# Keeping the last expert step's output rows in SBUF and fetching them by SBUF to SBUF transfers

## The reference, cut to what matters

```python
x = L0_attn_x                                        # (1, 8192, 512), f32
x = _layernorm(x + _L0_attn_ref(x, ...))             # long convolution by FFT; three earlier phases
x = _layernorm(x + _L0_ffn_ref(x, ...))              # this phase

def _L0_ffn_ref(x, controller, f1, bias, f2):        # 32 tokens per group, 128 experts (32 x 4)
    grouped = x.reshape(B, g, t, d)                  # 256 groups of 32 tokens
    logits = einsum('bgtd,des->bgtes', grouped, controller) + tie
    perm = (logits == max(logits, axis=-3))          # per group and expert: the one token it takes
    dispatched = einsum('bgtd,bgtes->bgesd', grouped, perm)
    inner = relu(einsum('bgesd,desf->bgesf', dispatched, f1) + bias)
    intermediate = einsum('bgesf,esfd->bgesd', inner, f2)
    return einsum('bgesd,bgtes->bgtd', intermediate, perm)   # "combine"
```

## Time and profile before

| | us |
|---|---|
| median of 3 runs | 2304.3 (2299.67 to 2306.85) |
| the profiled execution | 2312.54 |
| its span | 2310.7 |
| busy in the span: PE, DVE, ACT, POOL | 1933.4, 1387.6, 949.0, 440.1 |
| step 1, layers (part of it) | 1780 to 1838 |
| step 3, layers | 2062 to 2160 |
| late stage, loads issued to last combine | 2166 to 2302 |

### The profile page before, as it was taken

The page is one execution under the profiler, slowest core; times in us unless marked ns, Lnnn a source line. Parts: engine busy times, 40 slices in busy tenths (PEclk is TensorE's granted clock), DMA queues, the critical chain, the costliest instruction groups (busy, mean ns, idle before and its releaser), DMA issues. The chain is left out here.

```text
span 2310.7 us, 35055 instructions
## 1 busy us (share of the span) xinstructions
PE 1933.4 (84%) x12598; PEld 1322.0 (57%) x12598; DVE 1387.6 (60%) x2672; ACT 949.0 (41%) x1756; POOL 440.1 (19%) x279
## 2 busy tenths in 40 slices
PE   5999999999999699999769999994767676576444
PEld 5777777777777344444359988883636362252000
DVE  3878777777777255555458888882443354354344
ACT  3444444444444344444345555554323232242222
POOL 1100010011000044444345554540000000000000
PEclk9999999999999799999979999996888887686655
DMA  4134233423332578888587777756797999989999
GB/s 144 65 110 136 102 110 110 142 101 110 117 130 92 174 202 222 221 220 223 160 258 239 243 245 225 238 185 240 251 398 270 393 345 407 406 302 409 372 392 341
DMA packets 300365, 522.65 MB, mean 226 GB/s; under 512 B 26943, under 2 KB 119263, under 8 KB 291874
## 3 DMA queue, kind: packets, MB, share of 16 engines
q1 hardware_dynamic: 290978, 503.63, 64.5%
q10 hardware_dynamic: 9216, 16.78, 1.9%
HBM read 314.50 MB, written 205.82 MB: 225 GB/s over the span
## 5 line engine op out<-in xcount | busy, mean ns | idle before, releaser
L89 PE MATMUL p_pu<-p_xT_high,p_win_high 128*128 128x512 f32 (+1 forms) x816 | 334.6, 410 | 23.7 <-POOL p_xT_low L84 23.5
L91 PE MATMUL p_pu<-p_xT_low,p_win_high 128*128 128x512 f32 (+1 forms) x816 | 318.3, 390 | 0.0
L90 PE MATMUL p_pu<-p_xT_high,p_win_low 128*128 128x512 f32 (+1 forms) x816 | 318.3, 390 | 0.0
L369 ACT ACTIVATE p_t<-p_pu,p_tbias,p_taps 128x512 f32<-128x512 f32 x192 | 149.4, 778 | 385.2 <-PE p_pu L91 384.1
L473 DVE SCALAR_TENSOR_TENSOR p_t<-p_halo,p_taps,p_t 128x128 f32<-128x128 f32 (+1 forms) x384 | 196.8, 517 | 137.0 <-ACT p_t L369 135.9
L473 DVE SCALAR_TENSOR_TENSOR p_t<-p_pu,p_taps,p_t 128x384 f32<-128x384 f32 (+1 forms) x384 | 210.2, 547 | 6.9
L751 POOL TENSOR_TENSOR q_y<-q_y 128x512 f32<-128x512 f32 x128 | 160.3, 1273 | 277.8 <-DVE q_y L778 277.8
L84 POOL TENSOR_TENSOR p_xT_low<-p_xT,p_xT_high 128x2048 fp32r<-128x2048 f32 (+1 forms) x17 | 77.2, 4541 | 626.0 <-ACT p_xT_high L79 626.0
L89 PEld LDWEIGHTS p_pu<-p_xT_high,p_win_high 128*128 128x128 f32 x816 | 155.0, 190 | 56.9 <-issue 29.4
L1427 DVE COPY e_taken<-e_pd 128x1024 f32<-128x1024 f32 x64 | 78.4, 1224 | 161.8 <-PE e_pd L1360 161.6
L91 PEld LDWEIGHTS p_pu<-p_xT_low,p_win_high 128*128 128x128 f32 x816 | 154.4, 189 | 34.6
(11 more groups left out here) (120 smaller groups left out, 3499.9 us busy)
## 6 DMA issues: line engine op xcount, KB each, us to landing
s_I<-e_out SPq DMA_DIRECT2D x64, 1024.0 KB, 8.2
s_SV<-p_sout SPq DMA_DIRECT2D x128, 256.0 KB, 2.0
q_av<-s_SV SPq DMA_DIRECT2D x64, 512.0 KB, 4.3
s_Z<-q_z SPq DMA_DIRECT2D x128, 256.0 KB, 3.2
o_zin<-s_Z SPq DMA_DIRECT2D x64, 512.0 KB, 3.6
e_ff<-in_L_ffn_f SPq DMA_DIRECT2D x64, 512.0 KB, 8.9
e_inter<-s_I SPq DMA_DIRECT2D x32, 1024.0 KB, 12.8
e_taken<-s_I SPq DMA_DIRECT2D x32, 1024.0 KB, 11.3
```

The source lines that it names most:

```text
L89: pe.matmul(out, a[0], b[0], start=start, stop=False)
L90: pe.matmul(out, a[1], b[0], start=False, stop=False)
L91: return pe.matmul(out, a[0], b[1], start=False, stop=stop)
L369: nc.scalar.activation(t[r][m % 2][:], pu[(W + n) % 3][:], ACT.Identity, bias=tbias[:, w:w + 1], scale=taps[:, w, 2:3]).then_inc(t_ok, 1)
```

## The change

The output rows of step 3 no longer go to `I`. `keep_out` copies them into `taken`, over the dispatched rows of the same quad, which layer 1 has read by then; `taken` has a new shape for this, [128, 16 quads, 2048], and the dispatched rows of a quad lie together in it. A partition of `taken` then holds, for one group, the rows of 64 experts, 128 KB.

A late tile takes the rows of the first 64 experts from `I` as before (`load_stored`, 512 KB, into partitions 0 to 63), and those of the other 64 by four transfers from SBUF to SBUF, one for each group: from the one partition of `taken` that holds the group to partitions 64 to 127, 64 rows of 2 KB, 128 KB. The four groups of a tile lie in four partitions that are 8 apart (`place`); so `keep_tile` writes a tile's four group columns 8 elements apart, in every step, and the loads from `I` take groups 8 rows apart.

The late slots can't be in `taken` any more. There are seven: the buffers `out`, `inter` and the weight buffers, with the selections in `pick` and the tokens in `res` and `xt`. Before them SP waits for the last combined tile's matmul and for all its stores to the output; ACT and DVE close tile 31 ahead of the late stage. For the first three late tiles the half from `I` is loaded in the middle of step 3's layers.

```diff
-        taken = sb("taken", [P, DT * EH * GH])
+        taken = sb("taken", [P, QH, 4 * D])
...
+        def place(t):
+            return slice(4 * SPREAD * (t % 4) + t // 4, 4 * SPREAD * (t % 4) + t // 4 + 3 * SPREAD + 1, SPREAD)
+        def of_tile(m):
+            at = place(m % TH)
+            return slice(m // TH * GH + at.start, m // TH * GH + at.stop, at.step)
...
-                sp.dma_start(inter[s][:], S["I"][4 * m:4 * m + 4].rearrange("g e d -> e g d")
+                sp.dma_start(inter[s][:], S["I"][of_tile(m)].rearrange("g e d -> e g d")
...
+            def load_stored(m):
+                s = (m - NT0) % NL
+                sp.dma_start(late[s][0:EH], S["I"][of_tile(m), 0:EH].rearrange("g e d -> e g d")).then_inc(late_in[s], 16)
             def load_late(m):
                 s = (m - NT0) % NL
                 if m >= NT0 + NL:
                     sp.wait_ge(c_ps, ONE + m - NL + 1)
                 tile, choice = inter_of(m)
-                sp.dma_start(tile, S["I"][4 * m:4 * m + 4].rearrange("g e d -> e g d")).then_inc(late_in[s], 16)
+                if m >= NT0 + NO:
+                    load_stored(m)
+                for g, p in enumerate(range(P)[place(m % TH)]):
+                    sp.dma_start(tile[EH:ES, g, :], taken[p:p + 1].rearrange("o i (e d) -> o (i e) d", e=4)
+                                 ).then_inc(late_in[s], 16)
...
-                    sp.dma_start(S["I"][g0:g0 + GH, 4 * q:4 * q + 4, :], out[n % NO][:]).then_inc(stored[n % NO], 16)
+                    if c < STEPS - 1:
+                        sp.dma_start(S["I"][g0:g0 + GH, 4 * q:4 * q + 4, :], out[n % NO][:]).then_inc(stored[n % NO], 16)
...
+                    if c == STEPS - 1 and i == QH // 2:
+                        for x in range(NO):
+                            sp.wait_ge(stored[x], stores_before(x, (STEPS - 1) * QH))
+                        for x in range(NO):
+                            load_stored(NT0 + x)
-            for x in range(NO):
-                sp.wait_ge(stored[x], stores_before(x, STEPS * QH))
-            for s in range(2):
-                sp.wait_ge(h_ps[s], ONE + STEPS * QH // 2)
+            sp.wait_ge(c_ps, ONE + NT0)
+            sp.wait_ge(tile_ps, ONE + STEPS * TH)
+            sp.wait_ge(o_ps, ONE + STEPS * QH)
+            for s in range(NR):
+                sp.wait_ge(res_st[s], ONE + 16 * NT0 // NR)
             for m in range(NT0, NT):
                 load_late(m)
...
-            copy(rows[:, :, :, t * 4:(t + 1) * 4].rearrange("p k e (h g) -> p (k e) h g", g=2),
-                 pd[:, n % ND].rearrange("p h k e g -> p (k e) h g")).then_inc(taken_ok[n % 2], 1)
+            copy(rows[:, :, :, :, place(t)].rearrange("p i k e (h g) -> p (i k e) h g", g=2),
+                 pd[:, n % ND].rearrange("p h i k e g -> p (i k e) h g")).then_inc(taken_ok[n % 2], 1)
...
+            if n < (STEPS - 1) * QH:
+                eng.wait_ge(stored[n % NO], ONE + n // NO * 16)
+                to = out[n % NO][:, 2 * b:2 * b + 2, :]
+            else:
+                to = taken[:, n % QH, 2 * b * D:2 * (b + 1) * D].rearrange("p (e d) -> p e d", e=2)
+            copy(to, po[b]).then_inc(o_ok[b], 1)
```

More of the change, by code:

```diff
@@ L1152, in experts_phase @@
     NT0 = NT // NH
-    NL = 8
-    LW = 5 * D + P
+    NL = 7
+    SPREAD = P // 16
     with ExitStack() as ctx:
@@ L1164, in experts_phase @@
         pick = [sb(f"pick{s}", [P, 2, 2 * EH]) for s in range(NP)]
-        ff = [sb(f"ff{s}", [P, 2, D]) for s in range(NF)]
+        weights = sb("ff", [P, NF, 2, D])
+        ff = [weights[:, s] for s in range(NF)]
         hid = [sb(f"hid{s}", [P, GH]) for s in range(2)]
@@ L1172, in experts_phase @@
         std = [sb(f"std{s}", [P, 1]) for s in range(2)]
-        pd = ctx.enter_context(nc.psum_tensor("e_pd", [P, ND, 2, DT, EH, 2], F32))
+        pd = ctx.enter_context(nc.psum_tensor("e_pd", [P, ND, 2, QH, DT, 4, 2], F32))
         pc = [ctx.enter_context(nc.psum_tensor(f"e_pc{s}", [P, D], F32)) for s in range(2)]
-        banks = pd[:].rearrange("p b h k e g -> p (b h) (k e g)")
+        banks = pd[:].rearrange("p b h i k e g -> p (b h) (i k e g)")
         po = [banks[:, 0:2, :], banks[:, 2:4, :]]
         ph = [banks[:, 4 + s, 0:GH] for s in range(2)]
-        rows = taken[:].rearrange("p (k e g) -> p k e g", k=DT, e=EH)
-        late = taken[:, 0:NL * LW].rearrange("p (s w) -> p s w", w=LW)
+        rows = taken[:].rearrange("p i (k e g) -> p i k e g", k=DT, e=4)
+        late = [t[:] for t in out + inter] + [weights[:, 2 * n:2 * n + 2].rearrange("p n a d -> p (n a) d") for n in range(2)]
+        late_take = [pick[s // 2][:, s % 2, :] for s in range(NL)]
+        late_own = [t[:] for t in res] + [t[:, a, :] for t in xt for a in range(2)]
         consts, eps_ok = sem("e_consts"), sem("e_eps_ok")
@@ L1209, in inter_of @@
                 return inter[m % NI][:], take[m % NI][:]
-            v = late[:, (m - NT0) % NL, :]
-            return v[:, 0:4 * D].rearrange("p (g d) -> p g d", g=4), v[:, 4 * D:4 * D + P]
+            return late[(m - NT0) % NL], late_take[(m - NT0) % NL]
         def res_of(m):
@@ L1216, in res_of @@
                 return res[m % NR][:]
-            return late[:, (m - NT0) % NL, 4 * D + P:5 * D + P]
+            return late_own[(m - NT0) % NL]
         def combined(c):
@@ L1323, in _ @@
                         load_tile(m + NI)
-            for x in range(NO):
-                sp.wait_ge(stored[x], stores_before(x, STEPS * QH))
-            for s in range(2):
-                sp.wait_ge(h_ps[s], ONE + STEPS * QH // 2)
+                    if c == STEPS - 1 and i == QH // 2:
[8 more added lines that the diff above has]
+                sp.wait_ge(res_st[s], ONE + 16 * NT0 // NR)
             for m in range(NT0, NT):
                 load_late(m)
-            for s in range(NR):
-                sp.wait_ge(res_st[s], ONE + 16 * NT0 // NR)
             for s in range(NL):
-                sp.wait_ge(late_st[s], ONE + 16 * (NT - NT0) // NL)
+                sp.wait_ge(late_st[s], ONE + 16 * len(range(s, NT - NT0, NL)))
         @block.gpsimd
@@ L1359, in dispatch @@
                             r = slice(h * 2 * GT, (h + 1) * 2 * GT)
-                            m = pe.matmul(pd[:, b, h, k].rearrange("p e g -> p g e"), x[r, a, k * P:(k + 1) * P],
-                                          chosen[r, a, :].rearrange("p (g e) -> p g e", g=2), start=True, stop=True)
+                            m = pe.matmul(pd[:, b, h, :, k].rearrange("p i e g -> p g i e"), x[r, a, k * P:(k + 1) * P],
+                                          chosen[r, a, :].rearrange("p (g i e) -> p g i e", g=2, e=4), start=True, stop=True)
                     m.then_inc(tile_ps, 1)
@@ L1372, in layer1 @@
                         m = pe.matmul(ph[s][r, :], ff[w][:, 0, k * P + e * EF:k * P + (e + 1) * EF],
-                                      rows[:, k, 4 * i + e, :], start=(k == 0), stop=(k == DT - 1))
+                                      rows[:, i, k, e, :], start=(k == 0), stop=(k == DT - 1))
                 m.then_inc(h_ps[s], 1)
@@ L1391, in combine @@
                 else:
-                    pe.wait_ge(late_in[(m - NT0) % NL], ONE + ((m - NT0) // NL + 1) * 32)
+                    pe.wait_ge(late_in[(m - NT0) % NL], ONE + ((m - NT0) // NL + 1) * 96)
                 if m >= 2:
@@ L1426, in keep_tile @@
                     eng.wait_ge(h_ps[s], ONE + c * QH // 2)
-            copy(rows[:, :, :, t * 4:(t + 1) * 4].rearrange("p k e (h g) -> p (k e) h g", g=2),
-                 pd[:, n % ND].rearrange("p h k e g -> p (k e) h g")).then_inc(taken_ok[n % 2], 1)
+            copy(rows[:, :, :, :, place(t)].rearrange("p i k e (h g) -> p (i k e) h g", g=2),
+                 pd[:, n % ND].rearrange("p h i k e g -> p (i k e) h g")).then_inc(taken_ok[n % 2], 1)
         def keep_out(eng, copy, b, n):
             eng.wait_ge(o_ps, ONE + n + 1)
-            eng.wait_ge(stored[n % NO], ONE + n // NO * 16)
-            copy(out[n % NO][:, 2 * b:2 * b + 2, :], po[b]).then_inc(o_ok[b], 1)
+            if n < (STEPS - 1) * QH:
[4 more added lines that the diff above has]
+            copy(to, po[b]).then_inc(o_ok[b], 1)
         @block.scalar
@@ L1452, in close @@
             def close(m):
-                if m:
+                if m and m != NT0:
                     finish(m - 1)
@@ L1467, in _ @@
                         close(m)
+            finish(NT0 - 1)
             for m in range(NT0, NT):
@@ L1525, in _ @@
                         normed(m)
+            scale(NT0 - 1)
             for m in range(NT0, NT):
```

## The result

The changed kernel took 2549.9 us (median of 4 runs, 2546.5 to 2554.9) against 2304.7: a ratio of 1.106, interval 1.104 to 1.108. I had forecast 2337, at most 2520. The sign was right; the loss is 245 us, seven and a half times the 33 that I forecast.

What follows compares the result with a forecast made beforehand. It took DMA traffic to bound step 3's layers and the late stage. From the profiled 2312.5 us, -30, 0, 0, -4 and +67 gave 2345.5; less 8.2 to the runs' median, 2337 us, range 2263 to 2520.

Steps and rivals of the forecast that it cites:

- What bounds the kernel: Step 3's layers and the late stage: DMA engines full, both as long as their bytes need.
- Part 1: Step 3's layers: removing 16 stores of 1 MB shortens them, -30 us, from -22 to -37.
- Part 2: Junction before the late stage: store wait gone, tile 31's output wait in its place, 0 us, from -2 to +5.
- Part 3: Copies into taken: single elements 8 apart cost nothing, 0 us, at most some +5.
- Part 4: Late stage: narrow transfers raise a tile from 4.26 to 6.4 us, +67 us; early half tiles -4 us.
- The term for width: Late stage: 64 partitions cost 1.05 us more per 256 KB, 4.2 us per tile if no other traffic fills the gap.
- C: Late stage: engines meet at one partition, transfer after transfer; 25 us per tile, 2930 us, chance 0.20 with everything above 2500.
- the floor of side by side: Late stage: a tile's four single-partition transfers run at the same time, at least 5.5 us per tile.
- the 25 us of one after another: Late stage: four transfers of 5.5 us in turn plus 2.9 us for the tile's other traffic.
- B: The forecast itself: contention in part in the late stage, 2337 us, own range 2298 to 2420, chance 0.45.
- Rival A: Late stage: single-partition transfers cost only their bytes, 4.26 us per tile, 2270 us (2281 if issues limit), chance 0.28.
- D: Step 3's layers: stores gone but no shorter, as PE and copies set the wait; 2367 us, chance 0.07.

Runs made afterwards that it cites:

- e3: Kernel before with only the new places of the groups, 8 apart in taken and in I; stores and late stage unchanged: 2320.1 us.
- e9: Kernel before without step 3's 16 stores and the waits for them, late tiles loading other rows of the same bytes: 2270.0 us.
- e14: Changed kernel with the halves from I of the first three late tiles loaded in the late stage: 2541.8 us.
- e1: Changed kernel, each SBUF to SBUF transfer reading 2 KB from each of 64 partitions, not 128 KB from one (wrong rows): 2366.2 us.
- e4: Kernel before with each late tile's 1 MB load from I split into two 512 KB loads to 64 partitions each: 2373.1 us.
- e6: Changed kernel with a tile's four groups in partitions t, t+32, t+64 and t+96, issued in that order: 2768.9 us.
- e12: Changed kernel with groups 32 partitions apart, issued in the order t, t+64, t+32, t+96: 2611.9 us.
- e7: Changed kernel with consecutive tiles taking their groups from the lower and the upper 64 partitions by turns: 2547.9 us.
- e2: Changed kernel with a tile's four groups in four neighbouring partitions in place of 8 apart: 2828.9 us.
- e8: Changed kernel with a tile's four single-partition transfers issued between its other loads: 2586.7 us.
- e5: Changed kernel with ACT issuing the transfers of a tile's third and fourth group on its own queue: 2503.6 us.

## Why the prediction was wrong

The sum, from the runs: layout +12 (e3), stores and their wait gone -35 (e9), the new wait at the junction +6, early halves +8 (e14; +4 by its trace), narrow destinations 32 x 2.07 = +66 (e1, e4), single sources 32 x 5.7 = +182 (e1). Together +239 of the 245 us measured. The two profiled executions lie 234 us apart (2546.54 against 2312.54), so the sum is good to some 10 us, not better.

**What bounds the kernel** held for the kernel before: e9 takes bytes out of the layers and they get shorter. In the late stage after the change the bytes no longer set the time, for hardly fewer take 2.8 times as long.

**Part 1** (-30, from -22 to -37): the mechanism was right, and the size for the stores alone: e9's layers are 29.5 us shorter. The changed kernel kept 22 of them, the small end of the range (4.7 us between quads, where I had named 4.2 as the sign), since three narrow loads went in front of the weights. I had counted these by their bytes, 1.6 MB or 4 us in the layers and -4 us in the late stage. They cost 8.2 us in the layers and saved 4.4 (e14), a net loss of 4 to 8 us.

**Part 2** (0): right. From the last copy to the first late issue 2151.03 - 2145.11 = 5.9 us, against 6.5 to 6.6 before. e9 has no wait there, which makes this wait's price the +6 of the sum. What I said of the first late tile is part of the 12.03 us per tile and was not measured apart.

**Part 3** (0, at most +5): wrong. "So stride costs nothing" rested on one row of 128 elements at distance 64 (347 ns), of another operation, that is not a copy of 1024 elements. The copies became 1.55 times as long on DVE and 1.9 times on ACT. "64 x 1.2 = 78 us fits in it" treated waiting summed over all stages as cover for each copy. It did cover most: in e3 the copies add 98 us of work to the two engines (120.9 against 78.4 and 120.1 against 64.3) and 12 to the time. By the time of step 3's first store e3 is 10.4 us late (2077.03 against 2066.64), while at step 1's it was only 2.2 us (1782.42 against 1780.19): most is lost in the dispatch of steps 2 and 3. From the last store of step 1 to the first of step 2 it takes 1913.14 - 1842.06 = 71.1 us against 1904.47 - 1837.44 = 67.0. There the combine's work lies on the same two engines, which would explain it; no run tests this.

**Part 4** is the step that failed: "I take 6.4 us per tile", measured 12.03. The term for width came out right (half of 4.2, that is 2.1; e4 2.0, e1 2.1), though no row had shown that it is half and not all. So my 6.4 is the time of a tile with wide sources (6.33 in e1), and the single source in effect stood in the sum at nothing. It costs 5.7 us per tile, 182 us in all. It was taken as hidden, with the reason that "seven slots and the queue let the engines be at different transfers at the same time". They do so hardly: the order of transfers within a tile changes its time from 18.7 to 13.9 us (e6, e12), the order of tiles nothing (e7). Nor does an engine that is a little ahead get further ahead, my argument against C. Four transfers of 4.7 us from four places took 5.7 us more than from wide sources. So the price is neither the floor of side by side, 5.5 us, nor the 25 us of one after another, but about a third of the way from the one to the other. I had both ends in the text and put the likeliest value at the low one. The range stopped at 2520, early in the gap between B (to 2420) and C (2930); all above 2500 had a chance of 0.20, under C. By my own sign, a late stage of over 280 us, the forecast was wrong: it is 385. **Rival A** fell, **D** too. **C** had the right mechanism (engines meet at one partition) and an overlap too few; with neighbouring partitions (e2) it comes nearly true.

## What to carry to other kernels

Where the DMA engines are full, count for each transfer how many partitions it reads and writes, not only its bytes: 1 MB into halves of 64 partitions cost 2 us more than into 128, and 128 KB out of one partition held the engines at some 28 GB/s while it ran alone. Here the bytes saved in one stage (35 us) did not pay for the narrow shape in another. And when two prices for an unseen operation lie far apart, the range must hold what lies between them, unless a row excludes it.

## What the runs showed of the hardware that I had not expected

- An engine's busy share does not tell what it moves: 0.86 at 131 GB/s in the changed kernel, 1.04 at 382 before.
- ACT and DVE copies of 1024 f32 to single places: with two of them in each 16 bytes nearly at full speed (1059 and 1228 ns), one per 16 bytes or farther 1.9 to 2.06 us. The Trainium skill, SBUF — State Buffer, section "Specifications (TRN2)", says that a cacheline is 16 bytes and wants two hits per line; here the border lies exactly there. Why 128 elements at distance 64 took no longer than 128 in one run stays open: at the 0.66 ns per element that the 1024 cost more, 85 ns more would have been due.
- Other loads between the narrow transfers made the tile 1.3 us slower (e8), and a second queue made it 1.5 us faster (e5). How many transfers an engine holds at once was not measured directly.
